# The second attention of a two-block transformer on one core: a fourth bank for the early maxima, and values that leave PSUM without their bias

## Time and profile before

| | |
|---|---|
| three timed runs | 1966.72, 1971.39, 1961.26 us, median 1966.72 |
| profiled execution | 1961.52 us, its span 1959.7 us |
| mean granted clock of TensorE | 0.985 |
| busy share of the span | PE 95%, DVE 73%, ACT 60%, POOL 60% |
| this block begins at | 1271.3 us |
| its first weighed sum at | 1298.86 us |

### The profile page before, as it was taken

The page is one execution under the profiler, slowest core; times in us unless marked ns, Lnnn a source line. Parts: engine busy times, 40 slices in busy tenths (PEclk is TensorE's granted clock), DMA queues, the critical chain, the costliest instruction groups (busy, mean ns, idle before and its releaser), DMA issues. The chain is left out here.

```text
span 1959.7 us, 31266 instructions
## 1 busy us (share of the span) xinstructions
PE 1864.2 (95%) x10576; PEld 1471.1 (75%) x10576; DVE 1429.8 (73%) x2312; ACT 1176.6 (60%) x1897; POOL 1173.6 (60%) x945
## 2 busy tenths in 40 slices
PE   6999999999999999999999699889999989999997
PEld 5778888888888888888888577654555546888886
DVE  7777888888888888888888644377777766655556
ACT  5666676666666766666666655257666765533333
POOL 3776776777777767867766665214434446554445
PEclk9999999999999999999999899989999999999999
DMA  7877777778677777777777420000000010110001
GB/s 210 278 256 265 269 269 280 256 270 283 246 271 275 264 260 258 268 283 259 269 271 260 159 87 1 2 12 4 4 4 4 2 49 25 41 41 25 17 1 44
DMA packets 195603, 310.68 MB, mean 159 GB/s; under 512 B 12080, under 2 KB 154160, under 8 KB 195504
## 3 DMA queue, kind: packets, MB, share of 16 engines
q1 hardware_dynamic: 195504, 309.39, 45.9%
HBM read 173.03 MB, written 136.31 MB: 158 GB/s over the span
## 5 line engine op out<-in xcount | busy, mean ns | idle before, releaser
L620 POOL TENSOR_TENSOR attn_probT_lo<-attn_probT_lo,attn_probT_hi 128x1024 fp32r<-128x1024 f32 x254 | 610.6, 2404 | 198.4 <-ACT attn_probT_hi L987 198.1
L1104 DVE STREAM_TRANSPOSE attn_turned_prob<-attn_prob 128x1024 f32<-128x1024 f32 x256 | 318.2, 1243 | 123.9 <-ACT attn_prob L977 65.2
L977 ACT ACTIVATE attn_prob<-psum,attn_neg_max 128x1024 f32<-128x1024 f32 x256 | 285.7, 1116 | 145.2 <-DVE attn_neg_max L1098 142.0
L1098 DVE TENSOR_REDUCE attn_neg_max<-psum 128x1 f32<-128x1024 f32 x256 | 305.8, 1195 | 18.6 <-PE psum L81 18.0
L987 ACT ACTIVATE attn_probT_hi<-attn_probT_lo 128x1024 fp32r<-128x1024 f32 x256 | 269.3, 1052 | 2.2 <-DMA attn_probT_lo<-attn_spill 2.1
L81 PE MATMUL psum<-attn_probT_hi,attn_v_hi 128*128 128x512 f32 x512 | 205.5, 401 | 21.9 <-POOL attn_probT_lo L620 20.2
L81 PE MATMUL psum<-attn_probT_lo,attn_v_hi 128*128 128x512 f32 x512 | 205.3, 401 | 0.0
L81 PE MATMUL psum<-attn_key_hi,attn_q_hi 128*128 128x512 f32 x512 | 200.6, 392 | 3.8 <-ACT attn_prob L977 2.2
L81 PE MATMUL psum<-attn_probT_hi,attn_v_lo 128*128 128x512 f32 x512 | 203.6, 398 | 0.0
L81 PE MATMUL psum<-attn_key_lo,attn_q_hi 128*128 128x512 f32 x512 | 201.9, 394 | 0.0
L81 PE MATMUL psum<-attn_key_hi,attn_q_lo 128*128 128x512 f32 x512 | 201.2, 393 | 0.0
(11 more groups left out here) (251 smaller groups left out, 4761.1 us busy)
## 6 DMA issues: line engine op xcount, KB each, us to landing
attn_spill<-attn_turned_prob SPq DMA_DIRECT2D x256, 512.0 KB, 4.5
attn_probT_lo<-attn_spill SPq DMA_DIRECT2D x256, 512.0 KB, 5.0
x_sb<-in_w_qkvo SPq DMA_DIRECT2D x30, 512.0 KB, 5.0
attn_v_all<-in_moe_w SPq DMA_DIRECT2D x24, 384.0 KB, 3.0
acc_sb<-in_x SPq DMA_DIRECT2D x4, 512.0 KB, 6.1
acc_sb<-in_bo SPq DMA_DIRECT2D x16, 128.0 KB, 6.9
x_sb<-in_x SPq DMA_DIRECT2D x4, 512.0 KB, 5.5
mlp_staged<-in_ffn_w SPq DMA_DIRECT2D x4, 384.0 KB, 4.9
```

The source lines that it names most:

```text
L620: engine.tensor_tensor(lo, f32(lo), f32(hi), ALU.subtract).then_inc(done, 1)
L977: nc.scalar.activation(prob[:, tile % 2, :].rearrange("p (b n) -> p b n", b=NSQ), by_key, ACT.Exp, bias=neg_max[:, tile % 2:tile % 2 + 1], ...
L1098: nc.vector.tensor_reduce(neg_max[:, tile % 2:tile % 2 + 1], scores(tile), AX.XY, ALU.max, negate=True).then_inc(max_ready, 1)
L1104: nc.vector.transpose(turned_prob[:, tile % 2, :], prob[:, tile % 2, :]).then_inc(turned, 1)
```

## The change

It has three parts. The first: until fill 35 the maxima take four banks in turn, 0, 1, 2 and bank 7, which is that of the weighed sums and free until the first of them; from fill 36 on there are three again. Each pair of fills waits for the fills that had its banks before (nothing for the first four), and the first weighed sum waits for the last fill in bank 7. The second: the four takings of the first batch's values move from VectorE to ScalarE, as plain copies, and those of the second batch are plain copies on VectorE. No taking waits for the constants any more. The third: GpSimd's `take_v` adds the bias, broadcast over the eight token tiles, in place of the multiply by one, and waits for the constants ahead of the first.

```diff
--- before.py
+++ after.py
@@ -2248,7 +2248,15 @@
         o_done, spread_done, y_split = (st.sem(n) for n in ("o_done", "spread_done", "y_split"))
         block = ctx.enter_context(nc.Block())
 
-        max_bank = lambda n: k.psum[:, n % MAX_BANKS, :]
+        sums_bank = MAX_BANKS + RING
+        first_fill, sums_fill = (fills_before[n] for n in (LEAD - FIRST, LEAD - 1))
+        bank_of_fill, fill_earlier, had = {}, {}, {}
+        for fill in range(first_fill, HALVES * HALF_FILLS):
+            turn = fill - first_fill
+            bank = (0, 1, 2, sums_bank)[turn % 4] if fill < sums_fill else turn % MAX_BANKS
+            bank_of_fill[fill], fill_earlier[fill], had[bank] = bank, had.get(bank), fill
+        last_in_sums_bank = had[sums_bank]
+        max_bank = lambda n: k.psum[:, bank_of_fill[n], :]
         ring_bank = lambda what: k.psum[:, MAX_BANKS + (turn_of[what] + RING_FROM) % RING, :]
 
         def score_bank(g, h):
@@ -2345,12 +2353,15 @@
                 m, tiles = half % passes, slice(batch_of(half) * ST, (batch_of(half) + 1) * ST)
                 if half % passes == 0:
                     pool.wait_ge(v_full, (batch_of(half) + 1) * V_USES)
+                if half == 0:
+                    pool.wait_ge(consts, 128)
                 if half >= 2:
                     pool.wait_ge(weighed, (half - 1) * QUADS)
+                own_bias = bias_v[:, m * HG * D1:(m + 1) * HG * D1].rearrange("p (h d) -> p h d", d=D1)
                 nc.gpsimd.tensor_tensor(
                     v[half % 2][:, :, :, half % 2 * D1:(half % 2 + 1) * D1],
                     v_all[:, tiles, m * HG * D1:(m + 1) * HG * D1].rearrange("p t (h d) -> p t h d", d=D1),
-                    one[:].unsqueeze(2).unsqueeze(3).broadcast_to([P, ST, HG, D1]), ALU.mult).then_inc(v_ready, 1)
+                    own_bias.unsqueeze(1).broadcast_to([P, ST, HG, D1]), ALU.add).then_inc(v_ready, 1)
 
             def hide_later(g):
 
@@ -2411,8 +2422,9 @@
                 if pair_of_fills and unit_packed(units[n]):
                     return
                 fill = half * HALF_FILLS + fills_before[n] + 2 * pair_of_fills
-                if fill >= MAX_BANKS - 1:
-                    pe.wait_ge(max_free, fill + 2 - MAX_BANKS)
+                earlier = [fill_earlier[fill + h] for h in range(2) if fill_earlier[fill + h] is not None]
+                if earlier:
+                    pe.wait_ge(max_free, max(earlier) + 1)
                 maxima(pe, half, n, pair_of_fills, [max_bank(fill + h) for h in range(2)])
 
             def scores(g, pair):
@@ -2433,6 +2445,8 @@
 
                 half, (c, kt) = g // QUADS, quads[g % QUADS]
                 q0 = queries_from(c, kt)
+                if g == 0:
+                    pe.wait_ge(max_free, last_in_sums_bank + 1)
                 if kt == 0:
                     if half * chunks + c:
                         pe.wait_ge(o_done, half * chunks + c)
@@ -2563,6 +2577,12 @@
                         exp(g + AHEAD, h)
                 for n, (kind, of, c, part) in enumerate(jobs(g)):
                     use = first_use[g] + n
+                    if kind == "v" and of == 0:
+                        t = of * ST + 2 * part
+                        act.wait_ge(misc_full, use + 1)
+                        nc.scalar.activation(v_all[:, t:t + 2, :], misc_bank(use).rearrange("p (t n) -> p t n", t=2), ACT.Copy).then_inc(v_full, 1)
+                        act.wait_ge(v_full, of * V_USES + part + 1)
+                        act.nop().then_inc(small_free(use), 1)
                     if kind == "project":
                         act.wait_ge(misc_full, use + 1)
                         take_projection(act, of, c, misc_bank(use))
@@ -2626,7 +2646,7 @@
                         norm.take_lo(dve, of, misc.unsqueeze(1), (part,))
                         dve.wait_ge(norm.lo_done, of * KC + part + 1)
                         dve.nop().then_inc(small_free(use), 1)
-                    elif kind == "v":
+                    elif kind == "v" and of:
                         take_v(of, part, use)
                     elif kind == "sums":
                         dve.wait_ge(misc_full, use + 1)
@@ -2648,11 +2668,8 @@
             def take_v(b, n, use):
 
                 t = b * ST + 2 * n
-                dve.wait_ge(consts, 128)
                 dve.wait_ge(misc_full, use + 1)
-                nc.vector.tensor_tensor(
-                    v_all[:, t:t + 2, :], misc_bank(use).rearrange("p (t n) -> p t n", t=2),
-                    bias_v[:].unsqueeze(1).broadcast_to([P, 2, C]), ALU.add).then_inc(v_full, 1)
+                nc.vector.tensor_copy(v_all[:, t:t + 2, :], misc_bank(use).rearrange("p (t n) -> p t n", t=2)).then_inc(v_full, 1)
                 dve.wait_ge(v_full, b * V_USES + n + 1)
                 dve.nop().then_inc(small_free(use), 1)
 
```

## The result

The changed kernel took 1962.09 us (median of 13 runs, 1954.02 to 1968.11) and the one before 1968.92 us (13 runs beside them, 1961.26 to 1974.59). The ratio, taken over all these runs and not from the two medians, is 0.9962, 95% interval [0.9946, 0.9977]: faster by 7.5 us, between 4.5 and 10.6. In a second comparison the ratio was 0.9970 [0.9952, 0.9987], 5.9 us. The forecast was a gain of 4.0 us and 1962.5 us. The profiled execution after had a span of 1960.4 us, 0.7 longer than that of before, and that is the first thing to explain.

The account below looks back on a forecast made before the run. TensorE, busy 95% of the span, bounds the kernel, so only its waits in the second attention's lead-in pay: -4.0 us there, all else nothing, from median 1966.7 to about 1962.5 us; range 1954.5 to 1969.5.

Parts of the forecast that it names:

- The chain of the lead-in: Second attention's start up to its first exp: fewer waits bring that exp from 1291.38 to 1287.35, 4.0 us (2.3 to 4.5).
- the 6.4 us to 1277.85: TensorE's lead-in work without waits, from 1271.45 through fills 22 and 23; before, these began at 1279.37.
- ScalarE's four copies: First batch's values in the lead-in, 0.60 us each, within ScalarE's waits: no cost; the fourth without cover 0.60.
- the wait ahead of the first weighed sum: New TensorE wait for fill 35's reduction, met about 6 us early: no cost; without cover 0.65 us.
- the copies of the second batch: VectorE copies these values instead of adding the bias: no change, bounds -0.3 and +0.3 us for four.
- GpSimd's add: Eight bias adds replace multiplies by one, taken as 1.28 us each: no cost, at worst 1.7 us for seven.
- rival B: Denser lead-in keeps TensorE's clock high over the projection: gain 5.6 us, median 1961; chance 0.20.
- My sign of error: Forecast would be wrong if the distance from first exp to span end grew by more than 2 us.
- Rival C: Slower: more low-clock spells inside the second attention, at most 1.7 us each; with four, median 1969.5; chance 0.07.
- Rivals A and D: A: only VectorE's constants wait goes, gain 2.5 us, 0.14; D: GpSimd's adds and ScalarE's last copy cost, gain 1.7, 0.07.

Follow-up runs that it names:

- delay: The changed kernel with 50 chained 128x128 copies on ScalarE ahead of the first exps (17.0 us); median 1978.8 us against 1962.4.
- values_only: The changed kernel with three banks for the maxima as before; time not told from that of before, first exp 21.54 us behind the block's first matmul.
- no_wait_only: The changed kernel with three banks and VectorE copying all values without bias or constants wait; time did not move from before, first exp at 18.44 us.
- table_early: The changed kernel plus a one-element exp at the block's start, drawing the table load into ScalarE's idle time; median 1960.69 us, ratio to before 0.9955.
- table_busy: The changed kernel plus a one-element exp at the block's start and four pairs of maxima matmuls repeated; 1961.75 us.
- values_look: Second trace of values_only, taken for its lead-in at the high clock; first exp gained 2.3 us over before, no time given.
- banks_look: Second trace of the kernel before with only the fourth bank added; first exp at 19.01 us, gain 0.9 us, no time given.

## Why the prediction was right, and where its size was off

- **The chain of the lead-in.** Each point, moved by the 0.95 us of the later start: fills 28 and 29 at 1281.25 (predicted 1281.3), table load at 1286.11 (1286.1), first exp at 1287.40 (1287.35), gain 3.98 us (4.0), weighed sum at 1295.1 (1294.9). One reading on the way was loose: the 6.4 us to 1277.85 hold the 0.5 of fills 22 and 23 themselves, so they end there, and the 1279.37 that it is held against is their start. Their start was foretold for 1277.35 by these terms and came at 1277.23; the sum is unharmed, since VectorE's reductions are counted from the end. The low clock in 1282 to 1284 of before had a small part: VectorE idled 0.3 us for fills computed in it.
- **ScalarE's four copies, the wait ahead of the first weighed sum, the copies of the second batch:** nothing, as predicted; the copies take 689 ns for 690.
- **GpSimd's add** takes 1285 ns, the value taken (1.28), and costs nothing: kernels with and without it lie on one line, within 1.0 us.
- **The sum's size.** The forecast was 4.0 us; the measured 7.5 and 5.9 have intervals of 4.5 to 10.6 and 2.6 to 9.5. The mechanism was right; the term that was mis-sized is the clock. The prediction counted it at zero in the sum, and as rival B at 1.6 us on one spell of the lead-in. Over many runs it is worth about 4 us, and 3.7 us came already with the fourth bank alone, which the prediction gave a part in the chain only. In the one profile of the changed kernel rival B did not even show. I had read the clock off one execution, in which before had 0.985, and its mean over 83 runs is 0.9826.
- **Luck in the time itself.** The median, 1962.09, is 0.4 us from the 1962.5 forecast, and that is luck. The forecast stood on a median of three runs, 1966.72, where thirteen gave 1968.92; these 2.2 us and the gain that was too small by about 3 cancelled. The range was also not the sum of its own terms: a shift of -7 to +2 with 4 either way around 1966.7 is 1955.7 to 1972.7, not 1954.5 to 1969.5. The measured time lies in both.
- **My sign of error** was that the stretch from the first exp to the end would grow by more than 2 us. In the profile of the changed kernel it did, by 3.7 from the exp and 3.5 from the weighed sum, and the sign misled: it is the clock's, as the line over 14 traces shows. Rival C, more spells in the second attention, is what happened in that execution, but not on average.
- **Rivals A and D** fell: the wait by itself gives 1.5 us to the first exp, and behind the first weighed sum no step gives anything back. Between the first exp and there the delay leaves it open.

What stays open, beside the two parts whose gain the runs don't show: where in the program the changed kernel saves its time at 1.2 GHz. Its 25 runs have 13 us less of it (2 x 6.6) than before. The kernels with the fourth bank or with repeats have mean clocks of 0.984 to 0.987, except delay with its 17 us of idle (0.9824); those with three banks and no repeats have 0.9825 to 0.9829. That points to a denser lead-in, and the lead-in can show how: the low clock that began at the MLP's end lasted 13.7 us in values_only and 6.8 to 10.2 in the four traces with four banks that had it. But single traces also differ by up to 21 us behind the lead-in, and 14 of them don't settle it.

## What to carry to other kernels

Rebuild the chain between two fixed points from rows (here a block's start and its first exp) and look at that distance before the span: between the two traces of the changed kernel it repeated to 0.02 us, where the span over its first 13 runs varied by 14. It does so only where the clock between the points is the same, and no_wait_only warns that a gain there may not reach the time. Then compare the mean granted clock over many runs, for here a change that removes TensorE's idle went with as much again through the clock. Don't add the gains of parts: two changes to one chain gave 2.3 and 0.9 us alone and 4.0 together.

## What the runs showed of the hardware that I had not expected

The same MLP tail went into the block at the low clock in 5 of 14 traces, and there the first exp came 2.8 us later (table_early for table_busy, 17.44 and 14.69, whose repeats don't lie ahead of it on the chain) to 3.9 us later (values_only for values_look). With the banks alone it was only 0.1 us later (19.01 and 18.95), but that other trace had a low spell of its own inside the lead-in. TensorE idled 1.38 us in the MLP's end and 1.4 to 1.5 before the block's first matmul whether the clock fell there (table_early, banks_look, values_only) or not (before, the changed kernel). A microsecond at 1.2 GHz in the second attention and behind it cost 0.33 us. Where TensorE is the limit it costs more: the six projection matmuls took 2.86 us at 1.2 GHz and 1.5 at 2.4, so 0.48 us per us. That part of the low time falls on waits would explain the difference, and is not shown. And the block's start, behind identical code, lay anywhere between 1270.8 and 1278.4 us. It goes with the time at 1.2 GHz in the 200 us ahead of it, with a correlation of 0.73 and 0.35 us per us, about the price found behind the lead-in (with the low time since the program's start the correlation is 0.4). That is half of this spread (0.73 squared); the other half these runs did not look into.
